# Sixteen-head attentions rebuilt: scores computed twice on row quarters, the second time with keys on partitions

## The chip, the cores and the metric

One core of one Trainium2 chip runs the whole program. The metric is the device time in microseconds of one execution. Names used below: PE is TensorE (PEld its weight loads), DVE is VectorE, ACT is ScalarE, POOL is GpSimd, SP is SyncE. SBUF is the on-chip working memory of 128 partitions, PSUM the eight accumulation banks of 512 float32 per partition that only PE writes.

## The reference, cut to what matters

Four layers; each adds a gated cross-attention and a gated mixture of experts to the residual stream `x` (8 batches, 256 rows, 256 columns), against a context of 8 times 77 rows. Layers 1 and 3 have attentions of 16 heads of width 16. Layer 1 adds one bias per key to its scores and has no bias in its projections; layer 3 has the biases of its projections and no key bias.

```
q = (layernorm(x) @ Wq (+ bq)) in 16 heads of 16;   k, v = the same of the context (77 keys)
scores = einsum('bqhd,bkhd->bhqk', q, k) / 4 (+ key_bias[:, None, None, :] in layer 1)
attn = softmax(scores, axis=-1)
x = x + tanh(g) * (einsum('bhqk,bkhd->bqhd', attn, v) @ Wo (+ bp))
```

## The kernel before, in words

Each stage is a block in which every engine has its own written-out list of instructions in order; engines meet only at semaphores (`wait`, `wait_ge`, `then_inc`). There is no planner: the order on each engine is the order of the calls. `multi_head_attention` (L866) serves layers 1 and 3. It runs over 8 batches of 2 tiles of 128 query rows.

For each tile, with queries on partitions: PE multiplies the transposed queries with a block-diagonal copy of the keys (`spread_keys`, L1221, on POOL, 128x1232 per batch and in two slots), four heads by 77 keys at a time (`scores`, L978; in layer 1 the key bias is added by a second matmul, L981). ACT copies the scores out (L1077), DVE takes the row maxima (L1153), POOL subtracts them (L1236), ACT takes the exponent (L1084). PE transposes the 16 blocks of probabilities (L991), ACT copies them out as bf16 (L1090) and DVE writes what bf16 left over as a second bf16 part (L1160). `attend` (L1003) multiplies both parts with both parts of the values, head by head, 48 small matmuls of 17 columns per tile, the 17th column of ones giving the sums. DVE takes the reciprocal of 16 sums (L1175) and scales (L1179); PE transposes the result (L1011), ACT copies it (L1096), `project_out` (L1019) multiplies by Wo, DVE adds to `x` (L1167) and takes the statistics of the next normalisation (L199, L202), POOL the power (L299 in layer 1, L231 in layer 3), DVE applies it (L235; in layer 1 twice, and L284 as well), PE transposes (L306), ACT copies (L317). The query projection of batch b+2 (L952) and the scores of batch b+1 are computed during batch b. ACT and POOL also split the expert weights into bf16 parts chunk by chunk (`feed.high`, L1966, and `feed.low`, L1972), fed by SP's DMAs.

Before the first batch, layer 1 projects the values of all batches (L962, copied by L1148) and both layers split the values into bf16 parts (L1106, L1191); SP copies each batch's parts to a fixed place. Layer 3's values are projected ahead, in the stage before (`vector_values`, L860), and layer 1's key bias is prepared in the stage before it (`vector_bias`, L819 to L826).

The two-way tiled matmuls in the attention of layer 2 are used in the argument: `scores` there (L1441) writes two banks from the two row halves of the array, and its `attend` (L1470) two column halves of the output.

Of the kernel before, what the change touches and what calls it, by code (L numbers as in the profile page):

```python
# [360 lines left out]
class Loads:  # L361
# [35 lines left out]

    def scalar_keys(self, act):
        pass
# [344 lines left out]
GROUP = 4  # L744
GROUPS = HEADS // GROUP
BIAS_STEPS = 9


class HeadsAhead(Loads):
# [4 lines left out]
    def __init__(self, chip, a, layer):  # L754
# [5 lines left out]
        self.head_of = self.place(a["head_of"], CHUNK_HEADS)  # L760
        if self.key_bias:
            self.bias = self.place(a["key_bias"].partition_broadcast(P), CTX)
        else:
# [7 lines left out]
        if self.values_ahead:  # L771
            self.v1 = chip.keep[0:KEYS, :, :].rearrange("p t d -> p (t d)")[:, 0:BATCH * HEADS * (HEAD + 1)].rearrange(
                "p (b h d) -> p b h d", b=BATCH, h=HEADS)
# [7 lines left out]
        self.bias_ready = sem("bias_ready")  # L781
# [6 lines left out]
    def start(self):  # L788
        self.chip.finished.extend(self.sems)
        return super().start()  # L790

# [22 lines left out]
    def vector_bias(self, dve):  # L814
        bias, rows = self.bias, self.bias_rows
        high, mid = self.bias_parts
        dve.wait_ge(self.loaded, 16 * len(self.copies))
# [39 lines left out]
    def vector_values(self, dve, twos):  # L857
        for n in twos:
            dve.wait_ge(self.v_projected, n + 1)
            dve.tensor_tensor(self.v1[:, 2 * n:2 * n + 2, :, 0:HEAD],  # L860
                              self.v_bank[n % 2].rearrange("p (b h d) -> p b h d", b=2, h=HEADS),
                              self.bv[:, :].rearrange("p (h d) -> p h d", h=HEADS).unsqueeze(1).to_broadcast(
                                  [KEYS, 2, HEADS, HEAD]), ALU.add).then_inc(self.v_ready, 1)


def multi_head_attention(chip, given, layer, gate, norm_args, feed, clear=None, areas=()):  # L866

# [7 lines left out]
    with ExitStack() as ctx:  # L875
        st = LentStage(chip, f"l{layer}x", ctx, areas)
        bank = chip.bank
        s_bank = [bank[:, 0, :], bank[:, 1, :]]
        p_bank = [bank[:, 2, :], bank[:, 3, :]]
        o_bank, q_bank, y_bank, n_bank = (bank[:, n, :] for n in (4, 5, 6, 7))  # L880
        norm = NextNorm(st, [n_bank], **norm_args(st))
        clearing = Clearing(st, clear, 16) if clear is not None else None
        w, head_of, ctxT = given.w, given.head_of, chip.ctxT
        kT, qT = given.kT, given.qT
        k_diag = st.sb("k_diag", [P, 2, KD * CHUNK_HEADS * KEYS])
        v1 = given.v1 if given.values_ahead else st.sb("v1", [KEYS, BATCH, HEADS, HEAD + 1])
        v_parts = [st.sb(f"v_{n}", [KEYS, BATCH, HEADS * (HEAD + 1)], BF16) for n in ("high", "low")]
        v_now = [st.sb(f"v_{n}_now", [KEYS, HEADS * (HEAD + 1)], BF16) for n in ("high", "low")]
        v_high_ready, v_split = st.sem("v_high_ready"), st.sem("v_split")
        v_placed = st.sem("v_placed")  # L890
        raw = st.sb("scores", [P, TPB, HEADS * KEYS])
        probs = st.sb("probs", [P, TPB, HEADS * KEYS])
        probsT = [st.sb(f"probsT_{n}", [KEYS, HEADS * P], BF16) for n in ("high", "low")]
        row_max = st.sb("row_max", [P, TPB, HEADS])
        inverse = st.sb("inverse", [P, HEADS])
        mixed = st.sb("mixed", [P, DIM])
        mixedT = st.sb("mixedT", [P, KD, P])
# [2675 lines left out]
```

## Time and profile before

| | us |
|---|---|
| median of 3 runs | 1232.77 |
| lowest, highest | 1232.34, 1233.2 |
| span of the profiled execution, first to last instruction | 1230.8 |
| difference of the two | 2.0 |
| PE busy over the span | 999.3 (81%) |
| DVE busy | 779.5 (63%) |
| ACT busy | 561.8 (46%) |
| POOL busy | 564.8 (46%) |

The profiled execution's own time is its span of 1230.8 us; the runs' median stands 2.0 us above it, for what lies before the first and after the last instruction. The page names the engine's share of the whole span; what a change in one stage is worth has to be read inside that stage, from the windows and the timeline. A matmul in float32 has two records of PE and two of PEld, one in bf16 has one of each. A record's length includes the way through the array, so successive records overlap and the step from start to start is what a matmul costs.

### The profile page before, as it was taken

To read this page: it belongs to the slowest core of one execution; us is meant where nothing else is said; L and a number is where in the kernel's file an instruction comes from. 1 tells how busy PE (TensorE), PEld (TensorE's weight loads), DVE (VectorE), ACT (ScalarE), POOL (GpSimd) and SP (SyncE) were. 2 spreads that over 40 slices of the span, in tenths; PEclk is the share of its full clock that TensorE was granted. 3 is DMA by queue.
4 is the path that set the end of the run, shared out by engine and by line. 5 is a ranking of instruction groups with operands and counts; after the bars stand their busy time and mean duration, and the time that the engine had idled before them with its cause. 6 is when DMAs were issued, how large, how long until landed. Compare 5 with 4: busy or idle time off the path is not lost. (4 is left out here: it accounts for less than half of the span.)

```text
span 1230.8 us, 26812 instructions
## 1 busy us (share of the span) xinstructions
PE 999.3 (81%) x8467; PEld 761.3 (62%) x8476; DVE 779.5 (63%) x1807; ACT 561.8 (46%) x1379; POOL 564.8 (46%) x717
## 2 busy tenths in 40 slices
PE   4887869987489999408999439899987779998998
PEld 3666749976357777307999324455665558886443
DVE  4575754545948998664555365456653748886776
ACT  2362324443247777343434046566641258884110
POOL 1373736766537776260010344667651147773200
PEclk9996879998689999558999758899996979997999
DMA  3364239964132121468777130000001000000000
GB/s 120 97 176 156 90 121 335 352 243 127 56 126 59 44 56 45 154 267 280 265 257 257 58 99 1 1 1 1 1 1 52 1 17 24 23 24 9 18 26 26
DMA packets 73547, 125.10 MB, mean 102 GB/s; under 512 B 15849, under 2 KB 44707, under 8 KB 73443
## 3 DMA queue, kind: packets, MB, share of 16 engines
q1 hardware_dynamic: 65859, 103.00, 25.3%
q0 software_dynamic: 7584, 20.72, 5.0%
q8 instruction: 64, 1.05, 0.4%
q14 instruction: 40, 0.33, 0.1%
HBM read 53.00 MB, written 24.64 MB: 63 GB/s over the span
## 5 line engine op out<-in xcount | busy, mean ns | idle before, releaser
L317 ACT ACTIVATE xnT<-bank 128x256 f32<-128x256 f32 (+1 forms) x112 | 41.5, 381 | 76.2 <-PE bank L306 75.2
L2995 POOL DMA_DIRECT2D l_results<-keep x23 | 12.5, 544 | 132.2 <-DVE keep L3102 132.2
L3362 PE MATMUL bank<-room,xnT 128*128 128x128 bf16 x1104 | 66.7, 221 | 0.0
L3374 PE MATMUL bank<-l_weights,room 128*128 x552 | 65.0, 273 | 1.7 <-DVE room L3402 1.7
L3362 PEld LDWEIGHTS bank<-room,xnT 128*128 128x128 bf16 x1104 | 64.9, 99 | 0.3
L2801 PE MATMUL bank<-room,l0r_placed 128*128 128x128 bf16 x936 | 61.6, 225 | 0.0
L1883 POOL TENSOR_TENSOR l2x_probs<-l2x_probs,l2x_inverse 128x333 f32<-128x333 f32 x64 | 49.1, 789 | 25.1 <-DVE l2x_inverse L1790 25.1
L2801 PEld LDWEIGHTS bank<-room,l0r_placed 128*128 128x128 bf16 x936 | 58.5, 101 | 0.6
L3374 PEld LDWEIGHTS bank<-l_weights,room 128*128 128x128 bf16 x552 | 52.7, 98 | 9.2 <-issue 2.4
L2586 PE MATMUL bank<-l0f_x_high,l_weights 128*128 128x256 bf16 x256 | 45.4, 298 | 14.0 <-PEq L2771 7.9
L1632 ACT ACTIVATE l2x_probs<-bank,l2x_neg_max 128x333 f32<-128x333 f32 x64 | 34.0, 536 | 41.9 <-DVE l2x_neg_max L1772 36.5
L3387 ACT ACTIVATE room<-keep 128x1024 bf16<-128x1024 f32 x23 | 24.3, 1057 | 60.8 <-DVE keep L3397 60.8
L132 PEld LDWEIGHTS bank<-gate_weights,xnT 128*128 128x128 f32 x256 | 45.8, 267 | 8.0 <-issue 7.3
L132 PE MATMUL bank<-gate_weights,xnT 128*128 128x8 f32 x256 | 44.3, 303 | 5.4 <-PEq L113 4.0
L978 PE MATMUL bank<-l3x_k_diag,room 128*128 128x308 f32 (+1 forms) x128 | 42.9, 466 | 5.7 <-POOL l3x_k_diag L1227 5.0
L1772 DVE TENSOR_REDUCE l2x_neg_max<-bank 128x1 f32<-128x333 f32 x64 | 29.2, 497 | 28.9 <-PE bank L1444 28.9
L1972 POOL TENSOR_TENSOR l_weights<-l_weights 128x768 bf16<-128x768 f32 (+1 forms) x16 | 26.7, 1669 | 41.3 <-ACT l_weights L1966 41.3
L1160 DVE TENSOR_TENSOR l3x_probsT_low<-bank,l3x_probsT_high 77x512 bf16<-77x512 f32 x64 | 41.2, 681 | 6.0 <-ACT l3x_probsT_high L1090 4.0
L991 PE MATMUL bank<-ident,l_weights 128*77 128x128 f32 x256 | 37.1, 282 | 9.6 <-DVE l_weights L1160 8.9
L3402 DVE SCALAR_TENSOR_TENSOR room<-keep,room 128x1024 bf16<-128x1024 f32 x23 | 28.2, 1225 | 26.1 <-ACT room L3387 26.1
L1236 POOL TENSOR_TENSOR l3x_probs<-l3x_scores,l3x_row_max 128x616 f32<-128x616 f32 x32 | 38.9, 1216 | 12.5 <-DVE l3x_row_max L1153 12.2
L3014 PE MATMUL bank<-ident,keep 128*128 128x128 f32 x46 | 9.5, 289 | 43.1 <-DMA keep<-l_rows 43.1
(453 smaller groups left out, 3156.5 us busy)
## 6 DMA issues: line engine op xcount, KB each, us to landing
xnT<-l_weights SPq DMA_DIRECT2D x23, 1024.0 KB, 5.3
l0r_placed<-l_weights SPq DMA_DIRECT2D x39, 512.0 KB, 4.6
l0w_staging<-in_L_ffn_weights SPq DMA_DIRECT2D x16, 480.0 KB, 3.7
l_weights<-in_L_ffn_weights SPq DMA_DIRECT2D x16, 384.0 KB, 3.2
room<-in_L_ffn_weights SPq DMA_DIRECT2D x12, 512.0 KB, 6.0
room<-l_rows SPq DMA_DIRECT2D x39, 128.0 KB, 4.2
l_results<-room POOLq DMA_DIRECT2D x39, 128.0 KB, 4.1
xnT<-in_L_ffn_weights SPq DMA_DIRECT2D x8, 512.0 KB, 7.4
```

The lines of the kernel that those rows point to most:

```text
L132: last = pe.matmul(self.out[:, t * EXPERTS:(t + 1) * EXPERTS], self.chip.xnT[:, k, t * P:(t + 1) * P], self.weights[:, k, :], start=(k == ...
L317: act.activation(self.chip.xnT[:, :, span(t, P)], bank[:, 0:DIM].rearrange("p (k n) -> p k n", k=KD), ACT.Copy).then_inc(self.copied, 1)
L978: last = pe.matmul(s_bank[g % 2][:, 0:width], qT[:, c, u * P:(u + 1) * P], keys, start=True, stop=not key_bias)
L991: last = pe.transpose(p_bank[g % 2][0:KEYS, h * P:(h + 1) * P], probs[:, u, at:at + KEYS], chip.ident[:, :])
L1160: dve.tensor_tensor(probsT[1][:, at], p_bank[g % 2][0:KEYS, 0:GROUP * P], probsT[0][:, at], ALU.subtract).then_inc(low_copied, 1)
L1236: pool.tensor_tensor(probs[:, u, at].rearrange("p (h k) -> p h k", h=CHUNK_HEADS), raw[:, u, at].rearrange("p (h k) -> p h k", h=CHUNK_HEADS),
L1632: act.activation(probs[:, s, :], s_bank[n][:, 0:L2_KEYS], ACT.Exp, bias=neg_max[:, s:s + 1], accum_out=total[:, s:s + 1]).then_inc(probs_r ...
L1883: pool.tensor_tensor(probs[:, s, :], probs[:, s, :], inverse[:, s:s + 1].to_broadcast([P, L2_KEYS]), ALU.mult).then_inc(probs_normed, 1)
L2586: last = pe.matmul(self.bank[:, c, branch * width:(branch + 1) * width], self.weights[w][:, at:at + P], x[:, s, k, :], start=(i == 1), sto ...
L2801: last = pe.matmul(bank[:, u, m * P:(m + 1) * P], placed.parts[w][:, q, at:at + P], x[:, u, k, :], start=(s == 1), stop=(s == PARTS * KD))
L3362: last = pe.matmul(h_bank[u][:, m * P:(m + 1) * P], placed.parts[w][:, u, at:at + P], x[:, u, k, :], start=(s == 1), stop=(s == PARTS * KD))
L3374: last = pe.matmul(bank[:, 2 + u, 0:DIM], h[:, u, c * P:(c + 1) * P], expert_part(split[:, w, :, :], e, KD * hidden_width + c * DIM, DIM), ...
```

## The change

Both sixteen-head attentions are rewritten; a step is now a batch of 256 query rows, not a tile.

- The keys are stored in pairs: a head's 16 rows and its neighbour's share a quarter of 32 rows, and `keys` holds for each chunk of 8 heads the keys with even heads' rows kept and odd ones' zeroed, then the reverse (128x154, POOL, three slots).
- `find`: scores with queries on partitions, four matmuls per chunk of 8 heads, one on each quarter of the rows, each into its own bank (bank 0 to 3). They serve only the maxima. DVE reduces all 16 heads of a tile at once from PSUM, negated (`maximum`), PE turns the maxima (`turn_max`), DVE copies them out (`copy_max`).
- `shift`: the scores again with keys on partitions (77 by 256 queries for a head), on the same four banks, and four more matmuls that add the negated maxima with a matrix of ones and zeros (`takers`). ACT takes the exponent of four banks at once (77x2048), in layer 1 with the key bias as its bias operand. Nothing is transposed or split into bf16 parts.
- `attend`: values (77x32, one head's 16 columns and 16 zeros) as weights, probabilities moving, outputs in four column quarters; four more matmuls with ones give the sums on the same partitions. DVE takes the reciprocal of 128x256 sums and multiplies 128x256, once per chunk, straight into the transposed form that `project_out` needs.
- The values stay float32 and are not split or placed by SP. `vector_values` writes every value column twice as wide with zeros between (the zeros are set by POOL); in layer 3 this is done in the stage before. `vector_bias` computes on all rows and multiplies with row marks.
- The loops over batches are written out.

```diff
 def vector_bias(self, dve):
-        chain(dve.memset(rows[:, :], 0.0))
         chain(dve.tensor_scalar(bias, bias, HEAD ** 0.5, None, ALU.mult))
         chain(dve.tensor_copy(high[:, :], bias))
-        chain(dve.tensor_copy(rows[0:1, :], high[0:1, :]))
+        chain(dve.tensor_scalar(rows, high[:, :], marks[0], None, ALU.mult))
         chain(dve.tensor_tensor(bias, bias, high[:, :], ALU.subtract))
         chain(dve.tensor_copy(mid[:, :], bias))
-        chain(dve.tensor_copy(rows[32:33, :], mid[32:33, :]))
-        chain(dve.tensor_tensor(rows[64:65, :], bias[64:65, :], mid[64:65, :], ALU.subtract))
+        chain(dve.scalar_tensor_tensor(out=rows, in0=mid[:, :], scalar=marks[1], in1=rows, op0=ALU.mult, op1=ALU.add))
+        chain(dve.tensor_tensor(bias, bias, mid[:, :], ALU.subtract))
+        chain(dve.scalar_tensor_tensor(out=rows, in0=bias, scalar=marks[2], in1=rows, op0=ALU.mult, op1=ALU.add))
 def vector_values(self, dve, twos):
+            for r in range(2):
+                out = self.v_pairs[:, n * HEADS:(n + 1) * HEADS, r, r * HEAD:(r + 1) * HEAD]
+                rows = self.v_bank[n % 2].rearrange("p (g r d) -> p g r d", r=2, d=HEAD)[:, :, r, :]
+                if self.key_bias:
+                    last = dve.tensor_copy(out, rows)
+                else:
...
+                    for i in range(2):
...
+                        last = dve.tensor_tensor(out[:, of, :], rows[:, of, :], bias, ALU.add)
...
+            def find(b, u):
+                if u == 0:
+                    wait(pe, q_ready, b)
+                    pe.wait_ge(keys_spread, KD * b + KD)
+                    wait(pe, probs_ready, KD * (b - 1) + 1)
+                else:
+                    pe.wait_ge(max_ready, TPB * b + 1)
+                for c in range(KD):
+                    at = span(c, PAIR)
+                    for j, rows in enumerate(quarters):
+                        last = pe.matmul(bank[:, j, at], qT[b % 2][rows, c, u * P:(u + 1) * P],
+                                         keys[rows, b % key_slots, at], start=True, stop=not key_bias)
+                    if key_bias:
+                        for j, rows in enumerate(quarters):
+                            last = pe.matmul(bank[:, j, at], ones[rows, :],
+                                             bias_rows[rows, span(b, KEYS)].unsqueeze(1).to_broadcast([QUARTER, 2, KEYS]),
+                                             start=False, stop=True)
+                last.then_inc(found, 1)
+            def shift(b, c):
+                if c == 0:
+                    pe.wait_ge(maxT_ready, b + 1)
+                    wait(pe, probs_ready, KD * b)
+                elif b + 1 < BATCH:
+                    pe.wait_ge(max_ready, TPB * (b + 1) + TPB)
...
+                for r in range(2):
+                    at = c * PAIR + r * KEYS
+                    for j, rows in enumerate(quarters):
+                        pe.matmul(bank[0:KEYS, j, span(r, SEQ)], keys[rows, b % key_slots, at:at + KEYS], qT[b % 2][rows, c, :],
+                                  start=True, stop=False)
+                    for j, rows in enumerate(quarters):
+                        last = pe.matmul(bank[0:KEYS, j, span(r, SEQ)], takers[rows, 2 * c + r, :], neg_maxT[rows, :],
+                                         start=False, stop=True)
+                last.then_inc(shifted, 1)
+            def attend(b, c):
+                pe.wait_ge(probs_ready, KD * b + c + 1)
+                wait(pe, mixed_ready, KD * (b - 1) + c + 1)
+                for r in range(2):
+                    for j, rows in enumerate(quarters):
+                        pe.matmul(o_bank[c][rows, :], given.value_of(b, c * CHUNK_HEADS + 2 * j + r),
+                                  probsT[:, c, span(2 * j + r, SEQ)], start=(r == 0), stop=(r == 1))
+                for r in range(2):
+                    for j, rows in enumerate(quarters):
+                        last = pe.matmul(sum_bank[c][rows, :], summing[:, r, :],
+                                         probsT[:, c, span(2 * j + r, SEQ)], start=(r == 0), stop=(r == 1))
+                last.then_inc(attended, 1)
+            for b in range(BATCH):
+                ahead = BATCH - 1 - b
+                shift(b, 0)
+                if b >= 1:
+                    attend(b - 1, 1)
+                if b >= 2:
+                    norm.tensor(pe, TPB * (b - 2), 0)
+                if ahead >= 1:
+                    find(b + 1, 0)
+                if b >= 1:
+                    project_out(b - 1)
+                if b >= 2:
+                    norm.tensor(pe, TPB * (b - 2) + 1, 1)
+                if ahead >= 1:
+                    find(b + 1, 1)
+                attend(b, 0)
+                shift(b, 1)
+                if ahead >= 1:
+                    turn_max(b + 1)
+                if ahead >= 2:
+                    project_q(b + 2)
...
+            def exponents(b, c):
+                act.wait_ge(shifted, KD * b + c + 1)
+                wait(act, attended, KD * (b - 1) + c + 1)
+                act.activation(probsT[:, c, :].rearrange("p (j n) -> p j n", j=QUARTERS), s_banks[0:KEYS, :, :],
+                               ACT.Exp, scale=HEAD ** -0.5,
+                               bias=given.bias_columns[:, b:b + 1] if key_bias else 0.0).then_inc(probs_ready, 1)
...
+            def normalise(b, c):
+                n = KD * b + c
+                dve.wait_ge(attended, n + 1)
+                wait(dve, mixed_ready, n)
+                dve.reciprocal(inverse[:, :], sum_bank[c]).then_inc(inverse_done, 1)
+                dve.wait_ge(inverse_done, n + 1)
+                wait(dve, out_ready, b)
+                dve.tensor_tensor(mixedT[:, c, :], o_bank[c], inverse[:, :], ALU.mult).then_inc(mixed_ready, 1)
+            for b in range(BATCH):
+                if b >= 2:
+                    apply(b - 2)
+                if b >= 1:
+                    normalise(b - 1, 1)
+                if b + 1 < BATCH:
+                    for u in range(TPB):
+                        maximum(b + 1, u)
+                if b >= 1:
+                    update_batch(b - 1)
+                normalise(b, 0)
+                if b + 1 < BATCH:
+                    copy_max(b + 1)
+                if b >= 1:
+                    statistics(b - 1)
...
+            for b in range(BATCH):
+                if not key_bias:
+                    for u in range(TPB):
...
+                        pool.tensor_tensor(nth(chip.x, t), nth(chip.x, t), bo[:, :], ALU.add).then_inc(x_biased, 1)
+                feed.low(pool, b, 0)
+                if b + 2 < BATCH:
+                    spread_keys(b + 2)
+                feed.low(pool, b, 1)
+                if b >= 1:
+                    for u in range(TPB):
+                        norm.gpsimd(pool, TPB * (b - 1) + u, u)
```

On ACT the order within batch b is exponents(b, 0), the copies of the normalised rows of batch b-2 and `feed.high` twice, exponents(b, 1), the copy of the queries of batch b+2.

## Rows read from the trace of the kernel before

**Rows 1.** The page's first part: busy time, share of the span, instructions.
```profile
PE 999.3 (81%) x8467; PEld 761.3 (62%) x8476; DVE 779.5 (63%) x1807; ACT 561.8 (46%) x1379; POOL 564.8 (46%) x717
```

**Rows 2.** Windows in steady stretches of layers 1 and 3: length, then busy time per engine.
```profile
391.00:426.00 35.00, 33.14 (x356) 26.57 (x355) 32.23 (x57) 26.80 (x58) 25.29 (x29) 1.00 0.18 51
1030.00:1080.00 50.00, 50.00 (x575) 42.27 (x574) 42.56 (x80) 41.81 (x94) 38.09 (x47) 1.00 0.07 21
```

**Rows 3.** Timeline of PE (start, length): query projections of successive batches, layer 1, then layer 3.
```profile
425.78 1.89 PE L952 MATMUL bank<-xnT,room 128*128 x8
...
460.51 1.89 PE L952 MATMUL bank<-xnT,room 128*128 128x256 f32 x8
...
1060.17 1.89 PE L952 MATMUL bank<-xnT,room 128*128 x8
...
1075.32 1.89 PE L952 MATMUL bank<-xnT,room 128*128 x8
```

**Rows 4.** Timeline: start, first batch and end of layer 1's attention, then of layer 3's.
```profile
343.75 2.40 POOL L1227 TENSOR_TENSOR l_weights<-room 128x616 f32<-128x616 f32 x2 [6.26 <-POOLq L113]
...
360.15 1.10 PE L991 MATMUL bank<-ident,l_weights 128*77 128x128 f32 x8 [0.51 <-DVE l_weights L1148]
...
504.98 0.38 ACT L317 ACTIVATE xnT<-bank 128x256 f32<-128x256 f32 x1 [3.35 <-PE bank L306]
...
983.97 0.17 DVE L1139 MEMSET keep<- 77x128 f32 x1 [5.12 <-PEq L113]
...
997.40 1.10 PE L991 MATMUL bank<-ident,l3x_probs 128*77 128x128 f32 x8 [1.53 <-ACT l3x_probs L1084]
...
1128.17 0.38 ACT L317 ACTIVATE xnT<-bank 128x256 f32<-128x256 f32 x1 [3.35 <-PE bank L306]
```

**Rows 5.** Timeline of PE in layer 2's attention: matmuls on row halves and column halves.
```profile
845.31 0.83 PE L1441 MATMUL bank<-l2x_kT,l2x_qT 64*128 64x333 f32 x4
845.98 0.20 PE L1444 MATMUL bank<-l2x_mask_row,l2x_mask_one 64*128 64x77 bf16 x2
...
852.67 1.03 PE L1470 MATMUL bank<-l2x_probsT,l2x_v 128*64 128x256 f32 x8
853.64 0.66 PE L1428 MATMUL bank<-ident,l2x_qk 128*128 128x128 f32 x4
```

**Rows 6.** Reciprocals by line: duration ns min/median/max, first and last start, form.
```profile
L713 DVE RECIPROCAL l0x_scale<-l0x_total x16: 144/150/153, 42.9 to 97.2; 128x1 f32<-128x1 f32 x16
...
L1790 DVE RECIPROCAL l2x_inverse<-l2x_total x32: 151/164/167, 769.0 to 913.5; 128x2 f32<-128x2 f32 x32
...
L1175 DVE RECIPROCAL l3x_inverse<-bank x16: 224/256/259, 1008.4 to 1120.2; 128x16 f32<-128x16 f32 x16
```

**Rows 7.** Groups of DVE: busy us, mean ns, idle before.
```profile
L1772 DVE TENSOR_REDUCE l2x_neg_max<-bank 128x1 f32<-128x333 f32 x64 | 29.2, 497 | 28.9 <-PE bank L1444 28.9
...
L1167 DVE SCALAR_TENSOR_TENSOR x_res<-bank,gate,x_res 128x256 f32<-128x256 f32 x20 | 9.5, 473 | 3.3 <-PE bank L1019 3.3
...
L1179 DVE TENSOR_TENSOR l3x_mixed<-bank,l3x_inverse 128x256 f32<-128x256 f32 x16 | 6.8, 424 | 0.6
...
L700 DVE TENSOR_REDUCE l0x_neg_max<-bank 128x1 f32<-128x77 f32 x16 | 3.2, 229 | 4.1 <-PE bank L612 4.0
...
L860 DVE TENSOR_TENSOR keep<-bank,room 77x512 f32<-77x512 f32 x4 | 2.7, 683 | 1.0 <-PE bank L852 1.0
...
L823 DVE TENSOR_TENSOR room<-room,l0c_bias_high 128x616 f32<-128x616 f32 x1 | 0.8, 800 | 0.0
```

**Rows 8.** Groups of ACT reading PSUM.
```profile
L1090 ACT ACTIVATE l3x_probsT_high<-bank 77x512 bf16<-77x512 f32 x64 | 36.0, 590 | 6.5 <-PE bank L991 5.7
...
L1077 ACT ACTIVATE l3x_scores<-bank 128x308 f32<-128x308 f32 x64 | 26.5, 427 | 22.9 <-PE bank L978 21.8
```

**Rows 9.** Timeline of layer 1's last normalisation: end of statistics, power, application.
```profile
502.04 0.18 DVE L202 BATCH_NORM_AGGREGATE l_weights<-l_weights 128x2 f32<-128x6 f32 x1 [0.15 <-DVE l_weights L199]
...
503.75 0.42 DVE L235 TENSOR_SCALAR l_weights<-x_res,l_weights 128x256 f32<-128x256 f32 x1 [1.53 <-POOL l_weights L299]
```

More of the change, by code:

```diff
@@ new lines, in project_out @@
+            def project_out(b):
+                pe.wait_ge(mixed_ready, KD * b + KD)
+                wait(pe, q_ready, min(b + 2, BATCH - 1))
+                for u in range(TPB):
+                    for k in range(KD):
+                        last = pe.matmul(y_bank[u], mixedT[:, k, u * P:(u + 1) * P], w["Wo"][:, k, :],
+                                         start=(k == 0), stop=(k == KD - 1))
+                last.then_inc(out_ready, 1)
+            pe.wait_ge(consts_ready, consts)
+            find(0, 0)
@@ L1080, in exponents @@
-            def exponents(t, u):
-                for half in range(2):
-                    act.wait_ge(shifted, 2 * t + half + 1)
-                    at = span(half, 2 * width)
-                    act.activation(probs[:, u, at], probs[:, u, at], ACT.Exp,
-                                   scale=HEAD ** -0.5).then_inc(probs_ready, 1)
-            def high_probsT(t, g):
-                act.wait_ge(probs_transposed, GROUPS * t + g + 1)
-                wait(act, attended, t)
-                act.activation(probsT[0][:, g * GROUP * P:(g + 1) * GROUP * P], p_bank[g % 2][0:KEYS, 0:GROUP * P],
-                               ACT.Copy).then_inc(high_copied, 1)
@@ L1128, in _ @@
-            batches(act, batch)
-            copy_mixedT(TILES - 1)
+                wait(act, shifted, KD * (b - 1))
+                if key_bias:
+                    act.activation(qT[b % 2].rearrange("p k n -> p (k n)"), q_bank, ACT.Copy).then_inc(q_ready, 1)
+                else:
+                    for m in range(KD):
+                        last = act.activation(qT[b % 2][:, m, :], q_bank[:, m * SEQ:(m + 1) * SEQ], ACT.Identity,
+                                              bias=bq[:, m:m + 1])
+                    last.then_inc(q_ready, 1)
@@ new lines, in statistics, with apply @@
+            def statistics(b):
+                norm.vector_stats(dve, *((TPB * b + u, u) for u in range(TPB)))
+            def apply(b):
+                for u in range(TPB):
+                    norm.vector_apply(dve, TPB * b + u, u)
+                    norm.vector_apply_again(dve, TPB * b + u, u)
+            constants()
+            dve.wait_ge(max_cleared, 1)
+            for u in range(TPB):
+                maximum(0, u)
+            if not given.values_ahead:
+                given.vector_values(dve, range(2))
@@ L1216, in _, with spread_keys @@
+            apply(BATCH - 2)
+            normalise(BATCH - 1, 1)
+            update_batch(BATCH - 1)
+            statistics(BATCH - 1)
+            apply(BATCH - 1)
         @block.gpsimd
         def _(pool):
+            def spread_keys(b):
+                wait(pool, shifted, KD * (b - key_slots + 1))
+                for c in range(KD):
+                    pool.tensor_tensor(keys[:, b % key_slots, span(c, PAIR)].rearrange("p (r k) -> p r k", r=2),
+                                       kT[:, c, span(b, KEYS)].unsqueeze(1).to_broadcast([P, 2, KEYS]),
+                                       given.parity.unsqueeze(2).to_broadcast([P, 2, KEYS]),
+                                       ALU.mult).then_inc(keys_spread, 1)
```

439 lines of the change are left out of this document (135 added, 304 removed).

## The prediction

> **What bounds the kernel now.** I read the page's busy times first [rows 1]: PE is busy for 81% of the span, more than any other engine, but the page averages four layers and the change touches two stages. So I went to the windows of a steady stretch in each [rows 2]: in layer 3 PE is busy for 50.0 of 50 us, in layer 1 for 33.1 of 35, with DVE second (42.6 and 32.2) and the granted clock at 1.00 in both, the 2.4 GHz level. Then the timeline gives what one batch costs: the query projections follow each other by 15.15 us in layer 3 and by (460.51-425.78)/2 = 17.4 us in layer 1 [rows 3]. PE's own order bounds layer 3; in layer 1 DVE is nearly as full and PE waits a little for it. The two attentions run from 343.75 to 505.36 (161.6 us) and from 983.97 to 1128.55 (144.6 us); their first batches begin 16.4 and 13.4 us in [rows 4]. Both stages stand alone between barriers, so what they lose or gain goes to the end.
>
> **PE after the change, per batch.** Four float32 matmuls of 256 columns are 8 records of 1.89 us together; the last record's way out is 0.16, so one costs 0.43 us [rows 3]. Of matmuls on parts of the array the trace shows pairs [rows 5]: 8 records of 256 columns on two column halves take 1.03-0.16 = 0.87 us for four matmuls, and two of 333 columns on row halves take 0.67 where one after the other would be 1.12. Two at once is thus full overlap; four at once is not shown. Bounds: four in the time of one (0.43) or of two (0.87). I take 0.43, since the pair shows no loss at all.
> With that: shift twice, each 2x2 groups of four, 1.73 us: 3.46. Attend likewise 3.46. Find per tile: 154 columns are 0.26 us per group, two chunks 0.52 to 0.56, with layer 1's bias matmuls 0.75: 1.1 and 1.5 per batch. Query and output projection 1.73 each. Two turned maxima and four transposes at 0.23 (8 records in 1.10 less the tail [rows 4]): 1.35. Sum 12.85 (layer 3), 13.2 (layer 1). To it comes the change of tiling between whole array, row quarters and column quarters, nine times per batch. After the last record of L1470 (stream end 853.54) the next matmul starts at 853.64 and still has its weights to load [rows 5]; I take 0.2 us each, bounds 0 and 0.4: 1.8 us. PE's floor is 14.65 and 15.0 us per batch. The 32 probability transposes, 96 small matmuls and ACT's and DVE's bf16 copies all go, so the old work of the same size is traded for new, not just removed.
> The Trainium skill (TensorE: Matmul & The Clock Gate, Part 3, "Measured speedup vs the span model") has four row tiles of 512 columns at 3.07 times, not 4. By that each group takes 1.3 times as long. No run here shows four; it is a rival below.
>
> **DVE per batch.** Two maxima over 1232 elements of PSUM: 77 elements took 0.229, 333 took 0.497, so 1.05 ns each and 1.44 us [rows 7]. Two updates 0.87, copy of the maxima 0.42, two products 0.42 each [rows 7], statistics 1.2. The applications are 0.42 for layer 3's tile, 1.3 for layer 1's (three instructions of 0.4 to 0.5), each pair after 1.4 us of POOL's power (end of statistics 502.22 to 503.75 [rows 9]).
> The new cost is the reciprocal: 2 per batch of 256 elements, where it was 2 of 16. One element took 0.150, two 0.164, sixteen 0.256 [rows 6]. From 1 to 16 that is 7.1 ns per element, far over the 1.05 of the reduction; 256 make 0.15+255x7.1 = 1.96, so 2.0 us. Bounds: at one element per clock like the product, 0.42; at the slope from one element to the next two (14 ns, within the spread of these short rows) 3.7; I use 0.7 to 2.3, since sixteen elements fix the slope better.
> The Trainium skill (VectorE: DVE Perf Modes, "First, the fixed hardware budget") says the reciprocal is an iterative divide with a repeat count of 8. At the clock of 0.96 GHz in its specifications that gives, as an estimate, 256x8/0.96 = 2.13 us and the fixed part, 2.28, and the sum would lose 6 us of its gain. The slope of the rows is nearer to that than to one element per clock.
>
> **What lies on the path.** All of find and shift share four banks: exponents must end before find, maxima before the next find or shift. ACT's exponent of 77x2048: 0.8 ns per column from the two rows [rows 8], 1.8 us, beside PE's attend and transposes (2.6 with changes); it is covered, and would show only above 2.3. The first maxima lie beside output projection and transposes (2.4); the second beside attend(b,0) (1.9): covered. What is late is normalise(b-1,1). Counted from shift(b,0): shift ends 1.73, attend 3.66, DVE is told at 3.87. In layer 3 DVE is free; in layer 1 it began statistics 1.3 us before, then power wait and applications (1.2+1.4+2.6), free at 3.9. Reciprocal and product end at 6.3 to 6.4, while PE has done transposes and find by 5.1 (5.3): it waits at the output projection for 1.2 (layer 3) and 1.1 us (layer 1). Behind it stand find(b+1,1), attend(b,0) and shift(b,1), so the wait is on the path. DVE's rest (second reciprocal, copy of maxima) ends before PE's query projection does. Pitch: 14.65+1.2 = 15.9 (layer 3, before 15.15, slower) and 15.0+1.1 = 16.15 (layer 1, before 17.4, faster).
> Moved work: spread_keys, now 128x154 on POOL, memsets of zeros and feed.low have room, since POOL loses the subtraction of the maxima; SP loses the DMAs of the values. ACT loses all score and probability copies. All these are cover or slack: nothing on the path is gained there, and if POOL's power came late the applications would delay the reciprocal one for one.
>
> **Starts and tails.** Layer 1: keys 0.8, first find to 1.75, query projection to 3.7, second find (after the first maxima) to 4.6, 16 value matmuls 7.0, turn, copies: first batch at 13.6 instead of 16.4. Layer 3: find, maxima, find, maxima, turn, copy in series, 7.3 instead of 13.4; the 2 us split of the values and the wide key copy are gone. Batches 0 and 1 miss late work: 13.7+15.6 and 13.35+15.4. Batch 6 15.8 and 15.5. The tail from shift(7,0) is long, since it now ends a whole batch: two shifts, three attends, three reciprocals, statistics, two powers: 30.5 and 27.3.
> Layer 1: 13.6+13.7+15.6+4x16.15+15.8+30.5 = 153.8, 7.8 less. Layer 3: 7.3+13.35+15.4+4x15.9+15.5+27.3 = 142.5, 2.1 less.
> Outside: vector_bias gets one more instruction of 0.80 us and exchanges short ones for full width [rows 7], about +1.0, in a stretch where DVE is never idle. Layer 3's vector_values is four instructions of 128 elements (0.29 each) for one of 0.683 [rows 7], four times: +2.0, of which 1.5 counts, as DVE idles 0.5 before half of them. Bounds 0 and 3.5. Sum: -7.8-2.1+2.5 = -7.4. The profiled span of 1230.8 becomes 1223.4; the median lies 2.0 above, so 1225.
>
> **Rivals.**
> A, fast reciprocal: PE never waits for it; pitches fall to the floors and the tails by 3 x 1.3. At 0.7 us: layer 1 143.0, layer 3 132.4, in all -28: 1205. For it: nothing but the small number of elements seen. Against: 7.1 ns each.
> B, quarters overlap less than halves. Place: shift, attend, find, 8 us of PE per batch; there are 16 such groups of 256 columns per batch, so the gain of 7.4 us over 16 batches is gone once a group takes over 0.43+0.03 = 0.46 us. At 1.3 times: layer 1 168.5, layer 3 159.1, +24: 1257. At 1.5 times (two pairs, partly overlapped) 178.9 and 170.1, +45: 1278. At 2: +100: 1333. For it: each call has two records, and four tiles read four moving streams. Against: no loss in pairs.
> C, dearer changes of tiling and handoffs: 0.4 instead of 0.2 us adds 1.8 us per batch, 16 batches, +29: 1254; at 0.3, 1240.
> D, that the old order was covering more than I see (the written-out loops fetch more code, the cold start of PE): a few us, inside the range.
>
> **Chances.** Forecast (four at once, reciprocal 1.9 to 2.3) 0.50, its own range 1216 to 1236; A 0.15; B 0.20; C 0.15. No change means within 0.2%, 2.5 us, which is what a measurement can tell. Faster: 0.37 of the 0.50 and all of A, 0.52. Same: 0.09 and 0.01 of C: 0.10. Slower: the rest, 0.38. For 8 in 10: low end in A, 1204; high end in B and C, 1268.
>
> **What would show it.** In the changed profile: reciprocal rows of 128x256 at 2.0 us; four-quarter groups whose records start within hundredths of each other and step by 0.22; PE idle before the output projection, released by DVE's product, about 1.2 us; pitches of 15.9 and 16.15; first batches 13.6 and 7.3 us into their stages. The forecast is wrong if groups step by 0.29 or more, if the reciprocal is under 1.4, or if PE's gaps stand elsewhere than before project_out, at the exponents above all.

## The result, and the profile after

The changed kernel takes 1241.62 us (median of 8 runs, 1234.85 to 1245.6) beside 1232.67 for the kernel before on the same chip: ratio 1.0069, 95% interval 1.0043 to 1.0095. It is slower, where I had forecast 1225. A second measurement gave 1.0099 (1.0074 to 1.0123). The profiled execution has a span of 1239.6 us, 8.8 over the one before.

Its first part (busy time, share, instructions) answers to [rows 1]:

```profile
PE 989.8 (80%) x8764; PEld 714.5 (58%) x8764; DVE 724.5 (58%) x1679; ACT 451.8 (36%) x1050; POOL 465.7 (38%) x659
```

Every engine has less to do and the span is longer. The windows (start:end, length, busy of PE, PEld, DVE, ACT and POOL with counts, granted clock) give the steady stretches of [rows 2] first, then two new pairs for each stage: from its start to the query projection of batch 2, and from that of batch 7 to its end (q(2) and q(7) below). After:

```profile
391.00:426.00 35.00, 32.66 (x451) 22.13 (x447) 26.33 (x45) 16.07 (x16) 13.35 (x23) 1.00 0.18 48
1030.00:1080.00 50.00, 45.86 (x628) 30.36 (x620) 33.01 (x48) 21.07 (x29) 17.72 (x36) 1.00 0.06 18
...
345.21:377.31 32.10, 26.42 (x237) 16.91 (x237) 12.39 (x21) 4.37 (x5) 7.79 (x11) 0.71 0.44 144
986.63:1013.16 26.53, 19.66 (x172) 11.94 (x173) 9.38 (x12) 3.63 (x6) 6.60 (x13) 0.63 0.08 22
...
453.59:509.07 55.48, 46.83 (x444) 34.11 (x442) 30.49 (x61) 16.28 (x18) 15.67 (x28) 0.77 0.07 21
1087.71:1137.88 50.17, 41.96 (x428) 29.75 (x426) 24.69 (x45) 14.35 (x19) 11.31 (x24) 0.85 0.02 7
```

Before, the same four stretches:

```profile
343.75:374.89 31.14, 27.81 (x174) 19.08 (x175) 17.29 (x30) 16.42 (x32) 14.12 (x12) 0.95 0.42 138
983.97:1015.09 31.12, 23.22 (x126) 16.95 (x127) 13.66 (x20) 16.14 (x32) 14.96 (x14) 0.73 0.06 17
...
460.51:505.36 44.85, 40.00 (x438) 34.57 (x436) 35.77 (x71) 25.88 (x53) 25.04 (x32) 0.87 0.11 32
1090.39:1128.55 38.16, 36.74 (x429) 32.39 (x427) 28.54 (x57) 23.97 (x53) 20.85 (x30) 0.91 0.06 17
```

| us | start to q(2) | q(2) to q(7) | q(7) to end | stage |
|---|---|---|---|---|
| layer 1 before, after | 31.1, 32.1 | 85.6, 76.3 | 44.9, 55.5 | 161.6, 163.9 |
| layer 3 before, after | 31.1, 26.5 | 75.3, 74.5 | 38.2, 50.2 | 144.6, 151.3 |

That is the case: the steady batches win 9.3 and 0.8 us, layer 3's start 4.6, and the two tails give back 10.6 and 12.0. In the tails PE has about as many records as before (444 for 438, 428 for 429), but idles 8.7 and 8.2 us where it idled 4.9 and 1.4. It does the rest at a lower granted clock (0.77 for 0.87, 0.85 for 0.91), and its busy time grows by 6.8 and 5.2.

The executions of one kernel differ among themselves, and the longer ones tend to have the lower mean granted clock: the changed kernel's shortest, 1234.85 us, has 0.882, its longest, 1245.6, has 0.872. A trace shows one execution, so a stage time from it can be some us away from what the median stands for.

A steady batch of layer 3 in the timeline (start, length, engine):

```profile
1048.59 1.76 DVE L1142 RECIPROCAL l3x_inverse<-bank 128x256 f32<-128x256 f32 x1 [1.35 <-PE bank L1018]
1048.82 0.81 PE L975 MATMUL bank<-l3x_keys,room 32*128 32x154 f32 x16
...
1050.38 0.42 DVE L1145 TENSOR_TENSOR l3x_mixedT<-bank,l3x_inverse 128x256 f32<-128x256 f32 x1
...
1050.86 1.99 PE L1027 MATMUL bank<-room,l3x_mixedT 128*128 128x256 f32 x8 [1.23 <-DVE l3x_mixedT L1145]
...
1055.60 0.67 PE L1002 MATMUL bank<-l3x_qT,l3x_keys 32*77 32x256 f32 x8
...
1056.10 0.61 PE L1005 MATMUL bank<-l3x_neg_maxT,l3x_max_takers 32*77 32x256 f32 x8
...
1056.53 0.61 PE L1002 MATMUL bank<-l3x_qT,l3x_keys 32*77 32x256 f32 x8
...
1056.96 0.61 PE L1005 MATMUL bank<-l3x_neg_maxT,l3x_max_takers 32*77 32x256 f32 x8
...
1057.77 1.89 PE L961 MATMUL bank<-xnT,room 128*128 128x256 f32 x8
```

Three things are to be seen. The four-quarter calls (8 records are four float32 matmuls, one on each quarter) follow each other by 0.43 us, so four run in the time of one. PE stands 1.23 us before the output projection, for DVE's product. The reciprocal is 1.76 us. The next query projection starts at 1072.74, so the pitch, the step from one batch to the next, is 14.97. In layer 1 it is 438.36-423.11 = 15.25.

The tail of layer 1, the same view:

```profile
486.89 1.43 PE L1014 MATMUL bank<-l_weights 77*32 77x256 f32 x16 [2.08 <-ACT l_weights L1090]
...
492.66 3.78 PE L1027 MATMUL bank<-room,l_weights 128*128 128x256 f32 x8 [0.51 <-DVE l_weights L1145]
...
496.66 10.25 PE L132 MATMUL bank<-gate_weights,xnT 128*128 128x8 f32 x48
...
501.40 0.41 DVE L235 TENSOR_SCALAR l_weights<-x_res,l_weights 128x256 f32<-128x256 f32 x1
...
506.76 0.67 PE L306 MATMUL bank<-ident,l_weights 128*128 128x128 f32 x2
```

The last rows to be transposed are normalised at 501.8; PE comes to them at 506.76, because the gate matmuls (logits) of 12 tiles stand ahead in one burst. The code lets them begin only after the last exponent, since they write bank 0, which `shift` uses. Before, they lay between pieces of the last two tiles. The output projection takes 3.78 us, twice its 1.99.

### The profile page after: what moved, and what is told of

The parts are those of the page before. It is cut to its first block and busy times, and to the rows that moved or that the text cites. A ratio compares the mean times of both kernels' runs of the same rounds, so it can differ in the third digit from the quotient of the medians.

```text
span 1239.6 us, 25884 instructions
## 1 busy us (share of the span) xinstructions
PE 989.8 (80%) x8764; PEld 714.5 (58%) x8764; DVE 724.5 (58%) x1679; ACT 451.8 (36%) x1050; POOL 465.7 (38%) x659
## 5 line engine op out<-in xcount | busy, mean ns | idle before, releaser
L1090 ACT ACTIVATE l_weights<-bank,room 77x2048 f32<-77x2048 f32 x16 | 31.4, 1964 | 60.4 <-PE bank L1005 60.4
L132 PEld LDWEIGHTS bank<-gate_weights,xnT 128*128 128x128 f32 x256 | 48.7, 289 | 7.4 <-issue 7.1
L132 PE MATMUL bank<-gate_weights,xnT 128*128 128x8 f32 x256 | 47.7, 323 | 5.2 <-PEq L113 3.8
L1090 ACT ACTIVATE l3x_probsT<-bank 77x2048 f32<-77x2048 f32 x16 | 30.0, 1873 | 57.1 <-PE bank L1005 57.1
L1933 POOL TENSOR_TENSOR l_weights<-l_weights 128x768 bf16<-128x768 f32 x16 | 26.3, 1642 | 62.8 <-ACT l_weights L1927 62.8
L306 PE MATMUL bank<-ident,l_weights 128*128 128x128 f32 x64 | 17.6, 380 | 32.8 <-DVE l_weights L235 29.8
L2500 POOL DMA_INDIRECT l_rows<-keep,l0f_slot x32 | 31.3, 977 | 28.4 <-DVEq L2480 18.9
```

The source lines that it names most:

```text
L132: last = pe.matmul(self.out[:, t * EXPERTS:(t + 1) * EXPERTS], self.chip.xnT[:, k, t * P:(t + 1) * P], self.weights[:, k, :], start=(k == ...
L1090: act.activation(probsT[:, c, :].rearrange("p (j n) -> p j n", j=QUARTERS), s_banks[0:KEYS, :, :], ACT.Exp, scale=HEAD ** -0.5, bias=given ...
L2500: pool.indirect_dma_start(out=scratch.rows, out_offset=bass.IndirectOffsetOnAxis(ap=slot[:, t:t + 1], axis=0), in_=source[:, t, :], in_off ...
```

## The experiments

Times are medians; the ratios are to the kernel before, run beside each. Against it the full change is at 1.0069 and 1.0099. 0.1% is 1.2 us.

**One layer at a time.** Each kernel keeps the old attention, with its loads and values, in the other layer.

```diff
-        return HeadsAhead(chip, a, layer)
+        return (OldHeadsAhead if layer == 3 else HeadsAhead)(chip, a, layer)
-            multi_head_attention(chip, given, 3, 3, lambda st: {}, feed)
+            old_attention(chip, given, 3, 3, lambda st: {}, feed)
```

> Layer 1's attention in the new form, layer 3's in the old one (its values in the old layout too). Theory E (the loss stands at the edges of the two stages): in the traces layer 1's stage took 163.9 us after and 161.6 before, its start comes 1.5 us later for what is ahead of it, and the rest up to layer 3 is 1.0 shorter, so about 2.7 us over the kernel before: 1235.4. Inside it the pitch of the batches stays at 15.2 and the last query projection to the end takes about 55. Rival N (the new form as such pays in layer 1, where DVE was nearly full, and the loss is all layer 3's): 1228 to 1231. Rival X (a cost of the whole program, such as more code, split by neither stage): 1237 to 1241 here and in the other half too.

1228.24; 0.9957 (0.9934 to 0.9981). New in layer 1 alone the kernel is faster, as the rival N had it. Its trace does not place the gain in that stage: layer 1 takes 164.0 us there, as in the full change, and the span is 1.7 shorter than before because of what lies behind, the unchanged layer 3 (142.9) among it.

> Layer 3's attention in the new form, layer 1's in the old one. Theory E: layer 3's stage took 151.25 us after and 144.6 before, the rest behind it 0.5 less, so 6 us over the kernel before: 1239. The pitch inside it is 14.96 as in the full change (15.15 before). Rival X: 1237 to 1241 in both halves. If both halves add up to much more or less than the 9 us of the full change, the two are not independent. In this kernel every engine also waits once at the start of layer 1 for loads that are long in, which costs nothing.

1243.64, 1.0072; no measure of the half, since layer 1's keys, queries and bias were left out ahead of its stage. With them in place:

> Layer 3's attention in the new form, layer 1's in the old one (the kernel l3_new again; there layer 1's keys, queries and bias had not been computed ahead of its stage). Layer 1 alone in the new form measured 1228.2, 5.2 us under the kernel before, where the stage times of one trace gave +2.7; so those stage times are good to a few us only. Theory E (the edges, both stages): by the traces layer 3's stage is 6.7 us longer, 1239 to 1240. Theory L (the loss is layer 3's alone, and the two parts add up to the 8 to 9 us of the full change): 1246 or more. Below 1237: the two new stages together cost something that neither costs alone.

1246.89; 1.0100 (1.0072 to 1.0128). Within their intervals the parts add up (-0.43% and +1.00%, for +0.69 to +0.99%): by the medians the new form pays in layer 1 and costs more than that in layer 3, as theory L had it. The stage times of one trace had said +2 and +7. In this trace the unchanged layer 1 took 167.9 us (342.09 to 510.03) for 161.6, and the new layer 3 took 158.3 for 151.3 in the full change. Layer 1's windows, start to q(2), q(2) to q(7), q(7) to end:

```profile
342.09:376.92 34.83, 29.64 (x174) 20.64 (x175) 17.25 (x29) 16.62 (x32) 15.49 (x13) 0.90 0.37 123
376.92:462.57 85.65, 81.31 (x881) 65.45 (x880) 76.90 (x137) 66.19 (x140) 60.56 (x69) 1.00 0.19 52
462.57:510.03 47.46, 44.80 (x438) 39.49 (x436) 36.09 (x71) 26.01 (x53) 25.07 (x32) 0.74 0.11 30
```

The middle is the same as before to 0.03 us. The two ends have PE's records of before at a lower clock (0.90 for 0.95, 0.74 for 0.87) and are 3.7 and 2.6 us longer. A second trace of both kernels:

> The kernel before, unchanged, for a second trace of its stages. Layer 1's took 161.6 us in its first trace, and in the old form beside a changed layer 3 it took 167.9; layer 3's took 144.6 and 142.9. If one trace is good to 3 us, layer 1's stage is between 161 and 168 here; the cause of the scatter would be half-clock stretches of PE at the stage's two ends, not the pitch of the batches, which should be 17.4 and 15.1 within 0.2.

> The changed kernel again, for a second trace of its stages: 163.9 and 151.25 in the first one; here within 3 us of that, with the pitches of 15.24 and 14.96 unchanged and every difference at the ends. A median near 1242.

1232.87 (0.9998) and 1244.59 (1.0099). Stages before: 161.7 and 144.7, within 0.1 of the first trace; after: 163.8 and 151.3, likewise. The scatter I expected is not there in these two pairs. One trace of `l3_new_b` does not settle whether a stage costs more because another part of the program changed or because that execution's clock was lower (it is the longest of its four, 1248.72 us at 0.875, the shortest 1245.55 at 0.883). What the rows show is that the two ends differ, with their clock, and not the steady batches; how the loss divides between the layers is known from the medians alone.

**The burst of logits.**

```diff
+        chip.logits.out = m_bank[:, 0:TILES * EXPERTS]
...
+                if ahead == 0:                      # before shift(7, 0); again before project_out(6)
...
+                    chip.logits.some(pe, 4, norm)
...
+            chip.logits.some(pe, 4, norm)           # before attend(7, 1)
             attend(BATCH - 1, 1)
-            pe.wait_ge(probs_ready, KD * BATCH)
...
-            chip.logits.some(pe, 2, norm)
             project_out(BATCH - 1)
...
-            chip.logits.some(pe, TILES - TPB - 2, norm)
...
+            chip.logits.some(pe, 2, norm)
```

> The full change, with the gate matmuls (the logits, eight columns wide) written to the free half of bank 7 and put into PE's waits of the last batch: four tiles before shift(7,0), four before project_out(6), four before attend(7,1), two after the last project_out. In the changed kernel 48 of them stood in one burst of 10.25 us (layer 1) and 7.13 us (layer 3) between the last project_out and the last transposes. Theory E: the last rows are ready at 501.8 and 1132.9, and the transposes follow at once: layer 1's stage ends 6 us earlier, layer 3's 3.5 us, in all 1241.6-9.7 = 1232. Rival W (the burst is covered by the update, the statistics and the power anyway, and what is slow is the last batch itself): under 2 us gained, 1240 or more. Rival H (what costs is PE's half clock in the tail, and the fuller PE keeps 2.4 GHz): more than 12 us gained, below 1229, with project_out(7) at 1.99 instead of 3.78 us.

1234.04; 1.0002 (0.9979 to 1.0025): 0.7 to 1.0% under the full change, as theory E expected. Its trace, of an execution 2 us over the median, shows less of it than the 6 and 3.5 us forecast for the two stages: 160.3 for 163.9 and 149.8 for 151.3. Timeline of its layer 1:

```profile
493.62 3.78 PE L1028 MATMUL bank<-room,l_weights 128*128 128x256 f32 x8 [2.70 <-DVE l_weights L1154]
...
501.56 0.69 PE L306 MATMUL bank<-ident,l_weights 128*128 128x128 f32 x2 [1.39 <-DVE l_weights L235]
502.82 0.69 PE L306 MATMUL bank<-ident,l_weights 128*128 128x128 f32 x2 [0.57 <-DVE l_weights L235]
```

PE now waits for the rows, not they for PE. The output projection is still at 3.78 and layer 1's tail at 0.79 (0.77 before this edit), so the gain there is the order, not the clock. In layer 3's tail the clock rose too (0.89 for 0.85).

`warm_tail` is the full change with its burst in place; twelve tiles' gate matmuls are also done a second time, into a part of bank 7 that nobody reads, in PE's waits of the last batch.

> The full change; the burst of logits stays where it is, but twelve tiles' gate matmuls are also done a second time, to a part of PSUM that nobody reads, in PE's waits of the last batch (four tiles each before shift(7,0), project_out(6) and attend(7,1)). So PE has more to do and nothing is taken away. Theory E, where the burst itself is what is late: 0 to 1 us slower, 1241 to 1243. Rival H (the half clock in the tail is what costs): with the waits filled the clock stays up, project_out(7) takes 1.99 instead of 3.78 us and the burst 5.3 instead of 10.25, and 4 to 7 us are gained in layer 1 and 3 to 5 in layer 3: 1231 to 1235.

1244.61; 1.0075 (1.0049 to 1.0101): nothing gained. With most of the waits filled the projections of layer 1 stayed slow, only the burst was shorter:

```profile
478.36 3.76 PE L1027 MATMUL bank<-room,l_weights 128*128 128x256 f32 x8
...
494.88 3.49 PE L1027 MATMUL bank<-room,l_weights 128*128 128x256 f32 x8 [1.56 <-DVE l_weights L1160]
...
498.43 7.57 PE L132 MATMUL bank<-gate_weights,xnT 128*128 128x8 f32 x48
```

Rival H falls in that form: work put into these waits does not keep PE at the 2.4 GHz level in layer 1's tail. In layer 3 the clock of the tail was even lower (0.78 for 0.85), and its burst took 10.25 us for 7.13.

**The first batch.**

```diff
-                given.tensor_values(pe, range(2, 4))    # ahead of shift(0, 0)
...
                 if b >= 1:
                     attend(b - 1, 1)
+                elif given.values_ahead:
+                    project_q(2)
+                else:
+                    given.tensor_values(pe, range(2, 4))
```

(in layer 1, `project_q(2)` then stands before `find(1, 1)`.) `both` is `logits_gaps` with this edit. What it can fill, from the waits of PE in the changed kernel's layer 3, 986 to 1014 (total, times, longest); the second of these lies ahead of the first batch and stays:

```profile
PE bank L975 <- ACT l3x_probsT L1090: 2.1, 1, 2.1
PE bank L988 <- DVE l3x_neg_max L1129: 1.6, 1, 1.6
PE bank L975 <- DVE l3x_neg_max L1129: 1.6, 1, 1.6
```

> The kernel logits_gaps (1234.0) with the first batch filled too: in layer 1 the second half of the value projections goes from ahead of shift(0,0) to behind it, and the query projection of batch 2 ahead of the second find of batch 1; in layer 3 that projection goes behind shift(0,0). Theory E: what stood in series at the start of the stages now lies in PE's waits for the first exponent (2.2 us) and the first maxima (1.5 us): 3.1+1.5 us less in layer 1 and 1.9 in layer 3, 1234.0-6.5 = 1227.5. Rival H (the half clock at the start costs, not the waits; projections at half clock overrun the waits): 0 to 2 us, 1232 to 1234.

1227.60; 0.9943 (0.9921 to 0.9965): 0.6% under logits_gaps, the time that was expected. In layer 1's timeline the next find follows without a wait, where it waited 2.18 us for the exponent:

```profile
356.56 0.67 PE L1003 MATMUL bank<-room,l_weights 32*77 32x256 f32 x8 [1.12 <-DVE l_weights L1149]
...
358.45 3.68 PE L872 MATMUL bank<-room,ctxT 128*77 128x256 f32 x16
362.06 0.54 PE L976 MATMUL bank<-l_weights 32*128 32x154 f32 x8
```

The filled waits are not all of it. The windows of the first batch, from shift(0,0) to shift(1,0), in `logits_gaps` and then in `both`, layer 1:

```profile
359.01:378.12 19.11, 15.40 (x155) 9.21 (x155) 5.49 (x5) 5.39 (x4) 4.04 (x4) 0.64 0.15 42
356.56:371.82 15.26, 13.46 (x170) 8.87 (x171) 6.99 (x9) 5.53 (x5) 4.04 (x4) 1.00 0.25 77
```

PE is busy for less time although a set of value projections has been added, because the granted clock is 1.00 and not 0.64. In layer 3 the same windows are 18.97 us at 0.64 and 14.49 at 0.88. The second shift of the first batch shows it in every trace: 1.15 us for its first call where the batch is not filled, 0.67, the 2.4 GHz level, where it is. So here, unlike in the tail of layer 1, more work in the waits came with the higher clock, and the half clock that rival H names was part of the price of the start, though the filling did not overrun the waits as H had it. From the start of the stage to shift(1,0) the traces gain 7.1 and 4.4 us, for 4.6 and 1.9 expected from the waits; layer 3 gives some back at once, with an output projection of 3.46 us in its second batch, and more in its tail (48.7 us at 0.82 for 46.5 at 0.89).

**The reciprocal.**

```diff
-                dve.reciprocal(inverse[:, :], sum_bank[c]).then_inc(inverse_done, 1)
...
+                parts = 1 if c == 0 else TPB
+                for u in range(parts):
+                    at = span(u, SEQ // parts)
+                    dve.reciprocal(inverse[:, at], sum_bank[c][:, at]).then_inc(inverse_done, TPB // parts)
...
```

The product is cut in the same way, and each half of `project_out` waits for its own half.

> The full change with one edit: the reciprocal and the product of the second chunk are done in two halves of 128 queries, and each half of the output projection waits for its own. Theory R (the reciprocal is on the path, as predicted: PE stands 1.05 to 1.23 us before project_out in every batch): the first half is ready 1.0 us earlier, the second takes 0.3 longer, so PE waits 0.4 to 0.5 us in all, 0.6 to 0.8 less per batch, 14 batches and two tails: 1241.6-11 = 1230 to 1233. Rival S (the maxima behind it on DVE become late and PE waits for them at the second find instead): 0 to 4 us gained, 1238 to 1242.

1232.01; 0.9974 (0.9952 to 0.9995), 1.0 to 1.3% under the full change, as expected. Its layer 3:

```profile
1058.08 0.96 DVE L1145 RECIPROCAL l3x_inverse<-bank 128x128 f32<-128x128 f32 x1 [1.30 <-PE bank L1018]
...
1059.28 0.95 DVE L1145 RECIPROCAL l3x_inverse<-bank 128x128 f32<-128x128 f32 x1
...
1059.51 2.23 PE L1027 MATMUL bank<-room,l3x_mixedT 128*128 128x256 f32 x8 [0.39 <-DVE l3x_mixedT L1148]
...
1061.95 0.20 PEld L975 LDWEIGHTS bank<-l3x_keys,l3x_qT 32*128 32x128 f32 x4 [0.23 <-DVE l3x_neg_max L1129]
```

The wait falls from 1.23 to 0.39, two small ones come (0.40 at the second half, 0.23 at the maxima), and the pitch is 14.43. The price of the whole reciprocal, in a kernel that leaves the division out:

```diff
-                dve.reciprocal(inverse[:, :], sum_bank[c]).then_inc(inverse_done, 1)
+                dve.tensor_copy(inverse[:, :], sum_bank[c]).then_inc(inverse_done, 1)
```

> The full change with the reciprocal of the sums replaced by a copy of them (the division is left out, the product multiplies with the sums themselves). A copy of 128x256 from PSUM takes 0.41 us where the reciprocal takes 1.75. Theory R (PE's 1.05 to 1.23 us before project_out are the reciprocal's, and the three in each tail are in series): 14 waits of 1.05 to 1.23 and three times 1.3 us in two tails, 24 us less: 1217 to 1221; the pitch of layer 3 falls from 14.96 to 13.7. If something else ends just behind (the maxima before the second find): the pitch stays above 14.2 and the time at 1225 or more.

1212.36; 0.9826 (0.9794 to 0.9858): 2.4 to 2.7% less, 30 us and more. The pitch is what was expected, 13.66, and PE waits for nothing between 1013 and 1067:

```profile
1040.47 1.89 PE L961 MATMUL bank<-xnT,room 128*128 128x256 f32 x8
...
1054.13 1.89 PE L961 MATMUL bank<-xnT,room 128*128 128x256 f32 x8
```

The six us and more beyond the 24 expected are in the tails. Layer 3's takes 41.5 for 50.2 us, where three reciprocals in series are worth 4, an estimate from 1.3 each. Its granted clock is 0.96 for 0.85: the last output projection takes 1.98 for 3.78 us and the burst 6.02 for 7.13. The run thus prices the reciprocal together with what its absence did to the clock; layer 1's tail, 49.0 for 55.5 us, has its projections and its burst as slow as before (3.76 and 10.25).

**All together**, and with the old layer 3. `tuned` also swaps two lines on DVE:

```diff
-            apply(BATCH - 2)
             normalise(BATCH - 1, 1)
+            apply(BATCH - 2)
```

> The kernel both plus halves, and in the last batch DVE's last reciprocal ahead of the normalisation of batch 6 (it stood 1.5 us behind that in layer 1). If R and E hold and add up: 1227.5-9-1 = 1217 to 1220, below both kernels. If S holds: 1224 to 1228.

1220.38; 0.9888 (0.9863 to 0.9913). This beats both kernels, the one before by 1.1%. The edits add up in the main only: 1217 to 1220 was expected, and on top of `both` the halves and the swap gave 0.55%, where the halves alone had given 1.0 to 1.3%.

> Layer 1's attention as in the kernel tuned (new form, first batch filled, logits in the waits, reciprocal in halves), layer 3's in the old form. The new form alone measured -5 us in layer 1 and +12 in layer 3. In tuned's trace layer 3's stage takes 148.3 us against 144.6 and 142.9 for the old form, so if stages add up this is 4 to 5 us under tuned (1220.4): 1214 to 1217. If tuned's edits have taken away layer 3's loss altogether: 1219 to 1222.

1219.31; 0.9872 (0.9848 to 0.9896), not to be told from tuned: once the edges are mended, the new form costs layer 3 nothing that this measurement can tell. In the traces layer 3's stage takes 141.5 us here and 148.3 in tuned, but tuned's trace is of its longest execution, 1226.6 us at a mean clock of 0.880, 6.2 over its median; the trace here is of one at 1219.96 and 0.889.

## Why the prediction was wrong

By its own sum, in the profiled execution:

- **Quarters at full overlap: right.** Calls of four step by 0.43 us. The rule of the Trainium skill (TensorE: Matmul & The Clock Gate, Part 3, "Measured speedup vs the span model"), 3.07 times for four row tiles of 512 columns, would give a step of 0.56, an estimate; the trace does not agree. Rival B is out.
- **PE's floor: too high.** 14.65 was forecast for layer 3; without the reciprocal the pitch is 13.66. With the work at 12.85 that leaves 0.09 for each of nine changes of tiling, an estimate, not 0.2. Rival C is out as well, though its 1240 for 0.3 us a change comes near the measured time: that would have been luck.
- **Reciprocal: right in place, 1.75 for 2.0 us.** From 16 elements (0.256, [rows 6]) to 256 that is 6.2 ns each. The Trainium skill (VectorE: DVE Perf Modes, "First, the fixed hardware budget") with its repeat count of 8 gave 2.28, an estimate; measured is less. PE's wait is 1.23 and 1.05, forecast 1.2 and 1.1. That rival A's mechanism was worth something is shown by halves and no_reciprocal.
- **Pitches: better than forecast,** 14.97 and 15.25 for 15.9 and 16.15. From shift(1,0) to shift(7,0) that is 4.7 and 4.9 us in my favour.
- **Starts: the step that failed first, with everything priced at full speed.** I took 13.6 and 7.3 to the first batch and 13.7 and 13.35 for the first one itself. Measured: 15.3 and 9.5, then 19.1 and 18.8, together 7.1 and 7.7 us more. The prediction does not show how it came to 13.7 and 13.35; the rows of `both` show what is missing from them. There the first batch's own work, without the added value projections, steps through in 9.8 us in layer 1 at 2.4 GHz and would take 9.5 in layer 3, an estimate from its steps at that level. With the waits of the changed kernel (3.7 us for the exponent and the maxima in layer 1, 3.6 in layer 3) that makes 13.6 and 13.1, about what I had. The waits fit into the sum; the granted clock of 0.64 does not. It makes PE busy for 15.4 and 15.2 us, which accounts for the 5.4 and 5.5 missing in this batch. Ahead of it the clock was 0.81 and 0.68. The waits still matter, since with them filled the clock was 1.00 and 0.88.
- **Tails: the other step.** 30.5 and 27.3 from shift(7,0), measured 38.2 (470.89 to 509.07) and 33.3 (1104.55 to 1137.88): 7.7 and 6.0 more. The list had the shifts, attends, reciprocals, statistics and powers. It did not have the burst of logits, for which the last rows, ready at 501.8 and 1132.9, wait 5.0 and 2.7 us, nor the half speed: the last two output projections take 3.68 and 3.78 us in layer 1, 2.46 and 3.78 in layer 3, where they take 1.99 in the steady batches. It also does not say what it took for PE's wait for the last exponent (2.1 and 2.0 us).
- **Outside:** +2.5 forecast, -0.1 measured (8.8 less 2.2 and 6.7): the start of layer 1 is 1.5 later, what lies between and behind the two stages 1.6 shorter.

The edges cost 28.5 us more than forecast, the steady part 9.6 less, the outside 2.6 less: 16.2 in all, from -7.4 to +8.8. Rival D named "the old order was covering more than I see", with the cold start of PE, and gave it a few us; it was the largest term.

What is shown: the burst (0.7 to 1.0%), the first batch (0.6%), the reciprocal (1.0 to 1.3% by halving) are on the path, and mended together they turn +0.7 to +1.0% into -1.1%. Each of these edits moves work or shortens a wait, and in some stretches the clock moved with it; no run separates the two. What decides the clock is open. It rose in the filled first batches (0.64 to 1.00 and 0.88) and in layer 3's tail without the reciprocal (0.85 to 0.96). It hardly rose in layer 1's tail, with 0.77 in the full change, 0.79 in `logits_gaps` and 0.81 in `warm_tail`.

## What to carry to other kernels

A pipeline's steady pitch can be forecast to within 1 us from rows and still decide nothing when there are only eight batches: draw the first and the last batch as schedules of their own, and for each wait covered in the steady state ask what covers it there. A larger step (a batch for a tile) makes both edges longer, and work that used to fill them (the logits) needs a place again, for which its bank must be free. At the edges, price PE's records at the granted clock that the rows show there, and take a stage time from one trace only with that execution's time and clock beside its median.

## What the runs showed of the hardware

- Four float32 matmuls on four row quarters, or on four column quarters, take the time of one: steps of 0.43 us on rows and 0.44 on columns (0.89 for two calls, 457.46 to 458.35) at 256 columns. A change of tiling costs about 0.1 us, an estimate from the pitch of no_reciprocal (13.66 less 12.85, over nine).
- The reciprocal from PSUM takes 1.75 us for 128x256 and 0.95 for 128x128, 6.2 ns per element, where product and copy of the same size take 0.42.
- ACT's exponent of 77x2048 over four banks takes 1.87 us without and 1.96 with a bias per partition.
- Making PE busier in short waits left its projections at 3.76 and 3.49 us in layer 1's tail, where 3.78 is the 1.2 GHz level and 1.99 the 2.4 GHz level. In the first batch it came with a granted clock of 1.00 for 0.64.
- An unchanged stage took 161.6 and 161.7 us in two traces of one program and 167.9 in one trace of another, with the same steady batches and its two ends at a lower clock.
- Between executions of one kernel the time tends to go with the mean granted clock: 1234.85 us at 0.882 and 1245.6 at 0.872 for the changed kernel, 1217.06 at 0.890 and 1226.6 at 0.880 for tuned.
- That PE alone writes the PSUM banks is how this kernel uses them; no run here asks whether another engine can.
